# Feed-forward with FP4 blocks: the product of gate and up stays in PSUM, floor and scale as one operation, one tile multiplied back by VectorE, two gate banks

## What is computed

```python
def fp4_quant_dequant(x):              # blocks of 16 along the last dim
    scale = jnp.max(jnp.abs(xb), axis=-1, keepdims=True) / 6.0
    scale = jnp.maximum(scale, jnp.float32(1e-12))
    xn = xb / scale
    idx = jnp.searchsorted(_MID, jnp.abs(xn))
    q = _GRID[idx] * jnp.sign(xn) * scale
def fp4_linear(x, w):
    return jnp.einsum('bsk,nk->bsn', fp4_quant_dequant(x), fp4_quant_dequant(w))
gate = fp4_linear(x, w_gate)           # 128 -> 352
y = fp4_linear(x, w_up)                # 128 -> 352
h = jax.nn.silu(gate) * y
return fp4_linear(h, w_down)           # 352 -> 128
...
x = x + 0.5 * _L1_ffn_ref(_layernorm(x, axis=-1), ...)
```

## Time and profile before

| | |
|---|---|
| median of 3 runs | 708.93 us (707.54 to 710.84) |
| the profiled execution | 710.62 us |
| its span | 708.5 us |
| busy: PE, DVE, ACT, POOL | 646.7, 586.9, 451.9, 315.0 us |
| products `L1464` of `ffn_a`, first and last start | 393.53 and 484.53 us |
| products `L1464` of `ffn_b`, first and last start | 597.00 and 686.84 us |

### The profile page before, as it was taken

How to read it: one execution, slowest core, us unless ns; L and a number is a source line. 1 busy time by engine, 2 the same in 40 slices (tenths; PEclk the granted TensorE clock), 3 DMA queues, 4 the chain that set the end, 5 groups by cost and what they waited for, 6 DMA issues and landing times. The chain is left out here.

```text
span 708.5 us, 15987 instructions
## 1 busy us (share of the span) xinstructions
PE 646.7 (91%) x5778; PEld 464.9 (66%) x5778; DVE 586.9 (83%) x1540; ACT 451.9 (64%) x859; POOL 315.0 (44%) x424
## 2 busy tenths in 40 slices
PE   4999999999999989999999698998889987899895
PEld 3777777777878867777776366565565755556564
DVE  2788778966676679987889899999799998999983
ACT  3677779866456517777788466667655535667642
POOL 7100001185655422000012676745978675676520
PEclk9999999999999999999999799999999999999998
DMA  8100000000000000000000000000000000000101
GB/s 211 29 0 0 0 0 1 1 2 4 3 0 2 3 3 0 1 1 1 0 1 1 0 1 1 0 1 1 1 0 2 1 1 1 4 27 16 30 16 30
DMA packets 13464, 7.07 MB, mean 10 GB/s; under 512 B 1304, under 2 KB 13408, under 8 KB 13408
## 3 DMA queue, kind: packets, MB, share of 16 engines
q1 hardware_dynamic: 11328, 5.27, 2.8%
q10 hardware_dynamic: 2080, 1.05, 0.5%
HBM read 4.22 MB, written 2.10 MB: 9 GB/s over the span
## 5 line engine op out<-in xcount | busy, mean ns | idle before, releaser
L1546 PEld LDWEIGHTS ps<-expert_work 128*128 128x128 f32 x1024 | 132.6, 193 | 69.0 <-ACT expert_work L660 47.3
L1161 DVE SCALAR_TENSOR_TENSOR x_sb<-ps,gates,x_sb 128x128 f32 (+1 forms) x512 | 143.4, 342 | 30.2 <-PE ps L1546 22.1
L1546 PE MATMUL ps<-expert_work 128*128 128x128 f32 x1024 | 138.4, 278 | 1.0 <-ACT expert_work L660 1.0
L1546 PE MATMUL ps<-xnT,expert_work 128*128 128x512 f32 x256 | 135.1, 610 | 0.7 <-ACT xnT L641 0.7
L656 ACT ACTIVATE expert_work<-ps 128x512 f32<-128x512 f32 x128 | 75.6, 590 | 52.6 <-PE ps L1546 52.3
L367 POOL TENSOR_SCALAR vareps<-meanvar 128x4 f32<-128x4 f32 (+1 forms) x28 | 9.1, 324 | 222.2 <-DVE meanvar L1075 221.6
L660 ACT ACTIVATE expert_work<-expert_work 128x512 f32<-128x512 f32 x128 | 80.6, 630 | 4.1
L1546 PE MATMUL ps<-gateT,xnT 128*128 128x352 f32 x128 | 57.0, 528 | 14.6 <-ACT ffn_work L791 11.4
L424 POOL TENSOR_TENSOR shared<-shared 128x128 f32<-128x128 f32 x112 | 51.5, 460 | 24.9 <-ACT shared L751 16.7
L1546 PE MATMUL ps<-downT,hqT 128*128 128x128 f32 x384 | 57.2, 287 | 4.2 <-ACT hqT L901 4.0
L634 ACT ACTIVATE xn<-x_sb,shift,rstd 128x128 f32<-128x128 f32 (+1 forms) x132 | 55.4, 481 | 2.7 <-POOL shift L375 2.7
(11 more groups left out here) (180 smaller groups left out, 1330.0 us busy)
## 6 DMA issues: line engine op xcount, KB each, us to landing
x_sb<-in_L_attn_x_dram SPq DMA_DIRECT2D x8, 256.0 KB, 7.3
out_dram<-x_sb SPq DMA_DIRECT2D x8, 256.0 KB, 2.3
expert_work<-in_L_ffn_w_all_dram ACTq DMA_DIRECT2D x2, 512.0 KB, 6.5
wraw<-in_L_attn_qkv_w_dram SPq DMA_DIRECT2D x1, 192.0 KB, 4.5
wraw<-attn_in_proj_weight_dram SPq DMA_DIRECT2D x1, 192.0 KB, 3.4
fraw<-in_L_ffn_w_down_dram SPq DMA_DIRECT2D x1, 176.0 KB, 2.6
fraw<-in_L_ffn_w_gate_dram SPq DMA_DIRECT2D x1, 128.0 KB, 2.1
fraw<-in_L_ffn_w_up_dram SPq DMA_DIRECT2D x1, 128.0 KB, 2.1
```

The lines of the kernel that those rows point to most:

```text
L1161: t = nc.vector.scalar_tensor_tensor(tile_b(i, j), bank(4 + e % 4, TPB, C)[:, j, :], gates[:, j, e:e + 1], tile_b(i, j), ALU.mult, ALU.add)
L1546: return nc.tensor.matmul(o, a, b, start=start, stop=stop, **kw)
```

## The change

The product of silu and up is written in place over the four up banks. The maxima are taken from there, over 16 elements; one small operation sets the floor and multiplies by (1 + NUDGE)/6, and its result is both the reciprocal's input and the scale for multiplying back (`h_scale`, two buffers). So the divide is a plain product from PSUM, and `downT` no longer holds the 1/6. `EARLY` is 1: VectorE multiplies back tile 0 alone, POOL tile 1 in one operation and tiles 2 and 3 in a second. Gates alternate between banks 1 and 0 in all groups but the first. The first up of a group, and the first products of the attention, wait for the divide (`h_divided`) where they waited for the product.

```diff
--- before.py
+++ after.py
@@ -37,7 +37,7 @@
 BLK = 16
 NBH = 4 * FI // BLK
 KB = FI // BLK
-EARLY = 2
+EARLY = 1
 LN_EPS = 1e-5
 ATT_EPS = 1e-6
 MAGIC = 1.5 * 2.0 ** 22
@@ -178,8 +178,8 @@
         fq_h = fq_bufs("fq_h", 0, TPB * FI)
         fq_x = fq_bufs("fq_x", 5 * TPB * FI, TPB * C)
         silu_g = work(2 * TPB * FI, TPB * FI).rearrange("p (j f) -> p j f", j=TPB)
-        hid = work(3 * TPB * FI, NBH * (BLK + 1)).rearrange("p (k w) -> p k w", w=BLK + 1)
-        h_max = sb("h_max", [P, 2, NBH])
+        h_max = sb("h_max", [P, NBH])
+        h_scale = sb("h_scale", [P, 2, NBH])
         m_base = sb("m_base", [P, 1])
         warm = sb("warm", [P, 1])
 
@@ -266,9 +266,10 @@
         def tile_fb(g, j):
             return tile_f(False, g, j)
 
-        def late(a):
-
-            return a[:, KB * EARLY:NBH].rearrange("p (j k) -> p j k", k=KB).unsqueeze(3).to_broadcast([P, TPB - EARLY, KB, BLK])
+        def late(a, first, n):
+
+            return (a[:, KB * first:KB * first + KB * n].rearrange("p (j k) -> p j k", k=KB).unsqueeze(3)
+                    .to_broadcast([P, n, KB, BLK]))
 
         def early(a):
             return a[:, 0:KB * EARLY].rearrange("p (j k) -> p j k", k=KB).unsqueeze(3).to_broadcast([P, EARLY, KB, BLK])
@@ -283,6 +284,10 @@
         def v_bank(i):
 
             return 0 if i > 0 else 4
+
+        def gate_bank(j):
+
+            return 1 - j % 2
 
         def known_below(i, n):
 
@@ -383,7 +388,6 @@
             one(nc.gpsimd.memset(headsel[:, :], 1.0))
             one(nc.gpsimd.memset(headcols[:, :], 0.0))
             one(nc.gpsimd.memset(hq[:, :, FI:FK], 0.0))
-            one(nc.gpsimd.memset(hid[:, :, BLK:BLK + 1], 6e-12))
             one(nc.gpsimd.memset(m_base[:, :], BINADE))
             one(nc.gpsimd.iota(pos[:, :], pattern=[[1, T]], base=1, channel_multiplier=0,
                            allow_small_or_imprecise_dtypes=True))
@@ -476,8 +480,9 @@
                 def h_late(self, g):
 
                     pool.wait_ge(self.s["hq_ready"], g + 1)
-                    nc.gpsimd.tensor_tensor(hq_blocks(EARLY, TPB - EARLY), by_block(fq_h[0], EARLY, TPB - EARLY),
-                                            late(h_max[:, g % 2, :]), ALU.mult).then_inc(self.s["hq_late"], 1)
+                    for first, n in ((EARLY, 1), (EARLY + 1, TPB - EARLY - 1)):
+                        nc.gpsimd.tensor_tensor(hq_blocks(first, n), by_block(fq_h[0], first, n),
+                                                late(h_scale[:, g % 2, :], first, n), ALU.mult).then_inc(self.s["hq_late"], 1)
 
                 def x_back(self, g):
 
@@ -597,7 +602,7 @@
                 if m == 1:
                     a = nc.scalar.activation(upT[:, :], bank(1, FK), ACT.Copy, scale=-(1.0 - NUDGE))
                 if m == 2:
-                    a = nc.scalar.activation(downT[:, :, :], bank(1, 3, P), ACT.Copy, scale=-0.5 / 6.0)
+                    a = nc.scalar.activation(downT[:, :, :], bank(1, 3, P), ACT.Copy, scale=-0.5 * (1.0 - NUDGE))
                 a.then_inc(s_prep_act, 1)
 
             def x_squares(s, g):
@@ -784,6 +789,8 @@
                 a.then_inc(s["xn_ready"], 1)
 
             def silu(s, g, j, k=1):
+                if g > 0:
+                    k = gate_bank(j)
                 if j == 0 and g > 0:
 
                     act.wait_ge(s["hid_done"], g)
@@ -1456,25 +1463,27 @@
 
                 def body(g):
 
-                    h3 = hid[:, :, 0:BLK]
-                    largest = h_max[:, g % 2, :]
+                    hid = ps[:, 2:6, 0:FI].rearrange("p j (k w) -> p j k w", w=BLK)
+                    scale = h_scale[:, g % 2, :]
 
                     dve.wait_ge(s["up_done"], g * TPB + TPB)
                     dve.wait_ge(s["silu_ready"], g * TPB + TPB)
-                    nc.vector.tensor_tensor(h3.rearrange("p (j k) w -> p j k w", k=KB),
-                                            silu_g[:, :, :].rearrange("p j (k w) -> p j k w", w=BLK),
-                                            ps[:, 2:6, 0:FI].rearrange("p j (k w) -> p j k w", w=BLK),
+                    nc.vector.tensor_tensor(ps[:, 2:6, 0:FI], silu_g[:, :, :], ps[:, 2:6, 0:FI],
                                             ALU.mult).then_inc(s["hid_done"], 1)
                     if g == 0:
                         x_snap(s, 1)
                     dve.wait_ge(s["hid_done"], g + 1)
-                    ch.link(nc.vector.tensor_reduce(largest, hid[:, :, :], AX, ALU.max, apply_absolute_value=True))
-                    ch.link(nc.vector.reciprocal(h_inv[:, :], largest))
+                    ch.link(nc.vector.tensor_reduce(h_max[:, :].rearrange("p (j k) -> p j k", k=KB), hid, AX, ALU.max,
+                                                    apply_absolute_value=True))
+                    ch.link(nc.vector.tensor_scalar(scale, h_max[:, :], 6e-12, (1.0 + NUDGE) / 6.0,
+                                                    ALU.max, ALU.mult))
+                    ch.link(nc.vector.reciprocal(h_inv[:, :], scale))
                     if g > 0:
-                        dve.wait_ge(s["hq_late"], g)
-                    nc.vector.scalar_tensor_tensor(blocks(v), h3, 6.0 * (1.0 - NUDGE),
-                                                   h_inv[:, :].unsqueeze(2).to_broadcast([P, NBH, BLK]),
-                                                   ALU.mult, ALU.mult).then_inc(s["h_divided"], 1)
+                        dve.wait_ge(s["hq_late"], 2 * g)
+                    nc.vector.tensor_tensor(by_block(v, 0, TPB), hid,
+                                            h_inv[:, :].rearrange("p (j k) -> p j k", k=KB).unsqueeze(3)
+                                            .to_broadcast([P, TPB, KB, BLK]),
+                                            ALU.mult).then_inc(s["h_divided"], 1)
                     if g + 2 < GROUPS:
 
                         x_scales(s, ch, g + 2)
@@ -1491,7 +1500,7 @@
 
                         x_snap(s, g + 2)
                     ch.need(unbiased)
-                    nc.vector.tensor_tensor(hq_blocks(0, EARLY), by_block(v, 0, EARLY), early(largest),
+                    nc.vector.tensor_tensor(hq_blocks(0, EARLY), by_block(v, 0, EARLY), early(scale),
                                             ALU.mult).then_inc(s["hq_ready"], 1)
 
                 x_scales(s, ch, 1)
@@ -1568,13 +1577,18 @@
 
                 if j == 0:
                     pe.wait_ge(s["xnT_ready"], g + 1)
-                if g * TPB + j > 0:
-
-                    pe.wait_ge(s["silu_ready"], g * TPB + j)
+                if g > 0:
+
+                    k = gate_bank(j)
+                    if j != 1:
+                        pe.wait_ge(s["silu_ready"], g * TPB + j - (1 if j > 1 else 0))
+                elif j > 0:
+
+                    pe.wait_ge(s["silu_ready"], j)
                 mm(bank(k, FI), tok(j), gateT[:, 0:FI]).then_inc(s["gate_done"], 1)
                 if g > 0 and j == 0:
 
-                    pe.wait_ge(s["hid_done"], g)
+                    pe.wait_ge(s["h_divided"], g)
                 mm(bank(2 + j, FI), tok(j), upT[:, 0:FI]).then_inc(s["up_done"], 1)
 
             def keys_in(s, i):
@@ -1983,8 +1997,11 @@
 
             def ffn(s, first, front):
                 def hidden_transposes(g, j):
-                    if j == EARLY:
-                        pe.wait_ge(s["hq_late"], g + 1)
+                    if j in (EARLY, EARLY + 1):
+                        pe.wait_ge(s["hq_late"], 2 * g + 1 + j - EARLY)
+                    if j == 1 and g + 1 < GROUPS:
+
+                        pe.wait_ge(s["silu_ready"], (g + 1) * TPB + TPB)
                     for k in range(3):
                         t = nc.tensor.transpose(bank(6 * (1 - j % 2), 3, P)[:, k, :], hq[:, j, P * k:P * k + P], ident[:, :])
                     t.then_inc(s["htr_done"], 1)
@@ -2015,7 +2032,7 @@
                         pe.wait_ge(s["silu_ready"], GROUPS * TPB)
                         front.transposes_b(0, 0)
                         front.transposes_b(0, 1)
-                        pe.wait_ge(s["hid_done"], GROUPS)
+                        pe.wait_ge(s["h_divided"], GROUPS)
                         pe.wait_ge(s_par, 64)
                         pe.sem_inc(front.s["ctx_done"], B)
                         front.make_k(0, 0)
```

## The result

| | before | changed |
|---|---|---|
| median of 7 runs each | 709.71 us (707.45 to 711.02) | 713.41 us (711.26 to 714.44) |
| the profiled execution, its span | 710.62, 708.5 us | 711.26, 709.5 us |
| last interval between products in `ffn_a`, `ffn_b` | 12.38, 12.37 us | 11.72, 11.19 us |
| an interval in the middle of `ffn_b` | 12.69 us | 13.16 us |

The ratio of the runs is 1.0053, with an interval of 1.0035 to 1.0072: the change makes the kernel slower by about 3.7 us, where 706.5 was forecast and 709.8 was the top of the range. The profiled execution of the changed kernel was the fastest of its seven, while that of before (710.62) was slower than five of the seven in the table, so the two spans differ by 1.0 us only. What follows compares stretches of the two traces, and takes whole times from the ratios.

A forecast was written before the change was run, and what follows sets the result against it. VectorE was taken to bound 11 of 14 intervals between products; -2.0 - 0.6 + 0.3 - 0.1 = -2.4 us gave 708.2 by the profiled execution's clock, 706.5 us as median. Range: 703.5 to 709.8.

The forecast's parts named there:

- the third term of VectorE's list: VectorE's chain in one feed-forward group: floor and scale of 88 elements is new, 0.23 plus 0.03 wait, +0.26 us.
- Product, maximum, divide, multiplying back: VectorE's other operations per feed-forward group: product +0.015, maximum -0.09, divide 0, multiplying back -0.37 us.
- rival 3: PSUM as a source is dear: 0.06 us more on the maximum and on the divide, 707.8 us; chance 0.05.
- Sum per group: VectorE's list in one feed-forward group changes by -0.18 us, from 12.69 to 12.51.
- TensorE and the two gate banks: In each group two banks remove 0.83 us of silu holes; 0.9 us cover the first up's wait for the divide.
- its shut-out would end 0.3 sooner: POOL, shut out beside VectorE's long operations with two SBUF inputs, is free about 0.3 us sooner; x_back starts 0.47 later.
- rival 2: POOL sets the pace: transposes of x slip 0.3 us more, VectorE waits for the last up; 708.5 us, chance 0.14.
- The ends: Outside the 11 VectorE intervals: last interval of second stage -0.6, last of first stage +0.3, tail -0.1 us.
- the TensorE term: Last interval of the second feed-forward: TensorE loses the holes less the slip, 0.83 - 0.2, -0.6 us.
- Ahead of the attention the term: After the first feed-forward, ScalarE's normalised rows queue behind tiles waiting for POOL's first piece: taken as +0.3 us.
- the bound of 0.8: Before the attention, waiting for POOL's first piece costs between 0 and that piece's 0.8 us.
- Rival 4: Divide and x_back collide on a port: the divide waits 0.7 us per group, +5.3 us, 714.2 us; chance 0.05.

## Why the prediction was wrong

The step that failed is the third term of VectorE's list: "Floor and scale, 88 elements ... I take 0.23 ... +0.26." It measured 0.88. Both bounds of the term, 0.18 and 0.24, started from a row of the same kind of operation, `L1011`, which runs at 655.55 while POOL does nothing; the new one stands where POOL works. I had the operation's own price and not that of its place. The place was at hand: the maximum of 650.74 ends at 652.45, which is 665.14 one group later, and `L489` runs from 664.90 to 665.96. So was the price of a wait behind POOL: 0.78 us more for `L1487` in the earlier trace rows.

By the steps:

- **Product, maximum, divide, multiplying back:** 1.62, 1.62, 1.62 and 0.52 us. Confirmed, the reading of PSUM included; rival 3 fell.
- **Sum per group:** -0.18 forecast, +0.47 measured, -0.16 with the scale's source in PSUM. The whole difference is the scale.
- **TensorE and the two gate banks:** the holes went and the wait for the divide cost nothing, as forecast. The 5.6 us for four tiles were 4.84, since taking out the holes wasn't all: behind the first one the matmuls now start 0.59 us apart, where in the kernel before most stand 0.69 to 0.76 apart even without their holes.
- **POOL:** two pieces take 2.13 from start to end, 0.79 + 1.39 less the overlap: confirmed. That its shut-out would end 0.3 sooner is wrong: `L468`, at 663.65 in this group, still takes 1.33. So x_back, by the prediction's clock (the divide's end), came 0.73 us later and not 0.47: `L494` starts 10.78 after the divide's end of the group before, `L489` 10.05. It did no harm with two banks; rival 2 fell.
- **The ends:** the last interval of `ffn_b` gave 1.18 instead of 0.6 and the tail 0.94 instead of 0.1. In the interval the size of the TensorE term was too small: two gate banks alone gave 1.04 of it. The scale costs little there (0.28 and 0.20 at 680.90 and 692.09). In the tail 0.23 us were gained up to the transposes of tile 0 (11.25 us after the last product instead of 11.48), and 0.63 from there to ScalarE's last write (6.19 instead of 6.82). The granted clock is 0.50 where those transposes run and comes back behind them; the second tile's down products took 1.38 us in the kernel before and 0.83 in the changed one. So most of the tail's gain lies where TensorE's clock was back sooner, which no term forecast. Ahead of the attention the term was +0.3. TensorE at that place:

```profile
486.35 0.55 PE L2006 MATMUL ps<-ident,hq 128*128 128x128 f32 x3 [2.00 <-POOL hq L484]
...
491.44 1.06 PE L1862 MATMUL ps<-ident,xn 128*128 128x128 f32 x8 [0.45 <-ACT xn L639]
```

  The last interval of `ffn_a` was 0.66 us shorter, but the transposes of tile 1 waited 2.00 us for POOL's first piece (`L484` at 485.51). The attention's first products, `L1862`, start 7.78 us after the last product (483.66); those of the earlier trace rows start 6.53 after theirs. So the price at this place was 1.25 us, above the bound of 0.8, and with the 0.66 gained ahead of it +0.59 against +0.3.
- **Rival 4**, a collision of VectorE with x_back at 714.2 us, had the mechanism and the wrong instruction. It named the divide, which has one side in PSUM and doesn't collide, at "0.7 per group". I looked for a victim among the long operations and gave it 0.05. That its time was nearly met (713.4) is in part luck.

The collision has one size in all of these traces. An operation of VectorE that collides is longer by what POOL has left, less 0.13 to 0.14 us. Not every operation does, as the last three rows show:

| VectorE's operation | alone | beside POOL | longer by | POOL had left |
|---|---|---|---|---|
| scale, 654.60 | 0.20 | 0.88 | 0.68 | 0.81 |
| scale, 486.97 | 0.20 | 0.73 | 0.53 | 0.67 |
| scale, 475.25 | 0.20 | 0.28 | 0.08 | 0.21 |
| scale in the kernel before, 643.67 | 0.20 | 0.83 | 0.63 | 0.77 |
| divide with `EARLY = 1` alone, 646.34 | 1.62 | 2.26 | 0.64 | 0.78 |
| rounding, 466.43 | 1.63 | 2.41 | 0.78 | 0.92 |
| scale from PSUM, 652.71 | 0.25 | 0.25 | 0 | 0.81 |
| reciprocal in SBUF, 655.51 | 0.70 | 0.70 | 0 | 1.04 |
| divide with one side in PSUM, 656.25 | 1.62 | 1.62 | 0 | 0.30 |

The reciprocal also reads and writes SBUF and doesn't collide, so the place of the operands alone doesn't tell; the kind of operation counts too.

The Trainium skill's "SBUF — State Buffer", section "Who interferes with whom", has the rule that I read only in half. Its sentence on operations with at most one SBUF input excepts those in a 2-port perf mode, and it names `tensor_scalar` among the operations that can enter such a mode and contend; it also says that the engine that issues first blocks the other for its whole instruction. The table agrees up to the 0.14 us, in the direction where POOL was first. That the scale ran in such a mode is inferred; no row names the mode.

From 0.88 to 0.25 in eleven intervals are 6.9 us; between the changed kernel and the one with the maxima in PSUM the eleven intervals differ by 4.73 + 1.95 = 6.7.

What stays open: the rest of the time. The five stretches of the table come to +3.1 us and the medians differ by 3.7. With the first interval the sum is +2.0 in this pair of profiles, from which the clock in that interval took 0.5 to 0.65. So about 1 us of the medians' difference stands in no stretch; the ratio's interval reaches down to 2.5 us, so it may be noise. The profiled spans differ by 1.0 because the two starts differ by 0.99 as well, and that goes with the clock (above).

## What to carry to other kernels

Price a small operation from its place as well as from its kind: before it takes a row's duration, ask what GpSimd is running at the moment when it will start, and look for a row of the same kind of operation, with the same operand places, that met GpSimd. Where a short VectorE step in a chain waits for GpSimd, moving its source to PSUM can be enough: here it was 88 numbers per partition, 0.63 us per group and about 7 us in all. And resources show their worth in combination: two gate banks did nothing measurable in the kernel before and decided about 1% in the one with the maxima in PSUM and POOL's work in two pieces.

## What the runs showed of the hardware

- A short operation can wait longer than it runs: 88 elements in SBUF took 0.20 us with POOL idle and 0.88 beside POOL's 1.27 us operation; from PSUM, 0.25 beside the same operation.
- Reading PSUM costs 0.05 us more on this tiny operation, and nothing visible on 1408 elements (maximum and divide 1.62, where the divide from SBUF took 1.62).
- Whether VectorE collides with GpSimd depends on the operation too: the reciprocal of 88 elements in SBUF took 0.70 us beside a GpSimd operation and without one, where the scale on the same 88 went from 0.20 to 0.88.
- In stages that the change doesn't touch, TensorE's granted clock and the time went together: the first product started at 392.10 us with a mean clock of 1.00 from 150 to 300 us, and at 395.58 with 0.97.
